# A vision tower with a Fourier mixer and a routed MLP: the last step in its own order, and unread products in TensorE's gaps

## What is computed

```python
h = h + attn(layernorm(h))     # x_proj * mod, then a convolution along the tokens by rfft/irfft, then out_w
h = h + ffn(layernorm(h))      # base matrix + shared low rank + 2 of 6 routed experts of rank 16

# attn: x_proj = x @ in_w + in_b ; mod = gelu(x @ mod_w1 + b1) @ mod_w2 + b2
#       y = irfft(rfft(x_proj * mod) * rfft(kernel)) ; y @ out_w + out_b
# ffn:  gate = softmax(x @ router_W.T + router_b); the two largest, renormalised, weight the experts
```

## Time and profile before

| what | value |
|---|---|
| median of 3 runs | 1279.57 us (1276.67, 1279.57, 1279.72) |
| the profiled execution | 1276.65 us, its span 1274.9 us |
| PE busy | 1228.7 us, 96% of the span |
| DVE busy | 872.7 us, 68% |
| ACT, POOL busy | 585.6 us (46%), 400.0 us (31%) |
| DMA | mean 45 GB/s |

### The profile page before, as it was taken

One profiled execution on the slowest core, in us unless ns is written; L12 is line 12 of the kernel. 1 busy time (PEld: TensorE's weight loads), 2 busy tenths in 40 slices (PEclk: granted clock), 3 DMA queues, 4 the chain that ended last, 5 costly groups with the idle time before them and its releaser, 6 DMA issues.

```text
span 1274.9 us, 21132 instructions
## 1 busy us (share of the span) xinstructions
PE 1228.7 (96%) x8148; PEld 1204.5 (94%) x8148; DVE 872.7 (68%) x2617; ACT 585.6 (46%) x1108; POOL 400.0 (31%) x462
## 2 busy tenths in 40 slices
PE   6999999999999999999999999999999999999954
PEld 5999999999999999999999999999999999999954
DVE  6467766667766666776766776666677666667665
ACT  6644544444444435444544545444444444453410
POOL 4632333232233323223333223332322333232100
PEclk9999999999999999999999999999999999999976
DMA  7111111101111110111110011111011111100000
GB/s 239 38 38 51 50 51 38 50 17 47 50 51 51 38 50 13 51 50 51 50 39 29 35 50 51 51 38 51 14 51 50 51 50 38 49 15 13 13 1 33
DMA packets 23182, 57.18 MB, mean 45 GB/s; under 512 B 2665, under 2 KB 18218, under 8 KB 19114
## 3 DMA queue, kind: packets, MB, share of 16 engines
q1 hardware_dynamic: 22266, 55.05, 12.4%
q10 hardware_dynamic: 816, 0.79, 0.2%
HBM read 42.98 MB, written 12.85 MB: 44 GB/s over the span
## 4 chain that ended last, share of the span: by engine, by line
PE 94%; DVE 4%; DMA 1%; POOL 1%; ACT 0%; issue 0%; ACTq 0%; DVEq 0%; POOLq 0%
PE rotating L956 17%; PE rotating L957 17%; PE rotating L958 17%; PE rows_ps L956 10%; PE rows_ps L957 10%; PE rows_ps L958 10%; PE turn L1098 5%; PE turn L1082 2%; PE turn L995 2%; PE rows_ps L1003 2%; PE turn L956 1%; PE turn L957 1%; PE turn L958 1%; PE rotating L1063 1%; DMA spec_y<-dram_tok_w 1%; POOL w_l L349 0%
## 5 line engine op out<-in xcount | busy, mean ns | idle before, releaser
L472 ACT ACTIVATE gelu<-rotating,biases 128x392 f32<-128x392 f32 x256 | 148.9, 582 | 203.8 <-PE rotating L958 203.6
L383 POOL TENSOR_TENSOR folded<-modulated 128x196 f32<-128x196 f32 x64 | 38.6, 603 | 566.4 <-DVE modulated L794 566.4
L370 POOL TENSOR_TENSOR gelu_l<-gelu,gelu_h 128x784 fp32r<-128x784 f32 x62 | 117.2, 1890 | 227.6 <-DVE norm L777 201.4
L355 POOL TENSOR_TENSOR patches_l<-patches,patches_h 128x384 fp32r<-128x384 f32 x186 | 184.4, 1019 | 0.5 <-ACT patches_h L430 0.5
L956 PE MATMUL rotating<-gelu_h,w_h 128*128 128x392 f32 x512 | 177.7, 347 | 0.0
L956 PE MATMUL rotating<-x_h,w_h 128*128 128x392 f32 x512 | 177.2, 346 | 0.0
L957 PE MATMUL rotating<-x_l,w_h 128*128 128x392 f32 x512 | 174.6, 341 | 0.0
L958 PE MATMUL rotating<-x_h,w_l 128*128 128x392 f32 x512 | 174.6, 341 | 0.0
L957 PE MATMUL rotating<-gelu_l,w_h 128*128 128x392 f32 x512 | 174.3, 340 | 0.0
L958 PE MATMUL rotating<-gelu_h,w_l 128*128 128x392 f32 x512 | 174.0, 340 | 0.0
L956 PE MATMUL rows_ps<-tokw_h,patches_h 128*128 128x256 f32 x576 | 165.2, 287 | 7.4 <-POOL patches_l L361 7.4
(11 more groups left out here) (205 smaller groups left out, 2951.9 us busy)
## 6 DMA issues: line engine op xcount, KB each, us to landing
patches<-dram_x_rest SPq DMA_DIRECT2D x31, 1152.0 KB, 5.1
out<-h_sb SPq DMA_DIRECT2D x32, 384.0 KB, 2.5
patches<-dram_x_first SPq DMA_DIRECT2D x3, 384.0 KB, 4.8
h_sb<-dram_x_second SPq DMA_DIRECT2D x1, 768.0 KB, 8.2
prod<-dram_tok_w ACTq DMA_DIRECT2D x2, 256.0 KB, 5.5
gelu<-dram_w SPq DMA_DIRECT2D x1, 512.0 KB, 6.7
norm<-dram_w SPq DMA_DIRECT2D x1, 384.0 KB, 6.2
gelu<-dram_w SPq DMA_DIRECT2D x1, 384.0 KB, 7.3
```

The lines of the kernel that those rows point to most:

```text
L355: pool.tensor_tensor(patches_l[:, k, :], patches[:, k, :], patches_h[:, k, :].bitcast(F32), ALU.subtract).then_inc(pool_patches_lo, 1)
L370: pool.tensor_tensor(gelu_l[:, 2 * j:2 * j + 2, :], gelu[:, 2 * j:2 * j + 2, :], gelu_h[:, 2 * j:2 * j + 2, :].bitcast(F32), ALU.subtract)\
L383: pool.tensor_tensor(folded[:, m, 0, :, 1:NF], fwd, back, ALU.add)
L472: act.activation(gelu[:, k, :], bank(g + 1, UP[k])[:, 0:GT], ACT.Gelu, bias=b1_bias[:, k:k + 1]).then_inc(act_gelu, 1)
```

## The change

The loop ends with step 31. Step 32 and the end are written out, in another order on every engine:

- TensorE does two chunks of the first down product ahead of `inverse_dft(last - 1)` and two of the second ahead of `mixer_tiles(last - 1)`. DVE makes the first half of `modulated` ahead of `add_mixer(last - 1)` and the second in the middle of the layer norm (`meanwhile`), where both stood behind that norm. `turn_fold(last)` goes ahead of `turn_x2(last - 1)`, and `dft(last)` ahead of `base_route(last - 1)`. DVE's `gelu_lo` moves ahead of `spectrum_of_y` and `finish`.
- `gate_exp` is cut in two, `gate_range` (7 instructions) and `gate_exp` (7), and the parts of the gate of round `last - 1` are spread over waits. ACT makes the norm of the last two tiles (`last_normalise`).
- The last five tiles have one gate instead of two (a gate of three tiles and one of two), in memory of its own (`GateRoom`, in the `patches` buffer), for which two small constants are loaded. Their router and expert products (102 columns) are apart from the base products (256 columns) and ahead of them; the routed products add onto the base products in three banks, each stored when it is done.
- `keep_clock(ps, n)` makes n products of 512 columns into a free bank. Nobody reads them. There are 8, 4, 2, 3, 9, 24, 8, 6 and 5 of them at nine places, 69 in all.

The core of the diff (the gate's functions otherwise only take their memory as an argument):

```diff
-            for i in range(1, GROUPS + 1):
+            for i in range(1, GROUPS):
                 if i + 2 < ROUNDS:
                     load_patches(i + 2)
+                else:
+                    sp.wait_ge(pool_patches_lo, KT * (ROUNDS - 2))
+                    sp.dma_start(last_thr, last_rank_thr_d).then_inc(last_consts, 16)
+                    sp.dma_start(last_bias, last_router_bias_d).then_inc(last_consts, 16)
                 if in_range(i - 3):
                     store(i - 3)
-            for d in range(GROUPS - 2, ROUNDS):
-                store(d)
-            sp.wait_ge(result_out, 16 * ROUNDS)
+            last = GROUPS - 1
+            store(last - 2)
+            store(last - 1)
+            first = output_tiles(last)[0]
+            for n, tiles in enumerate(LAST_BANKS):
+                sp.wait_ge(dve_result, last + n + 1)
+                at, slot = first + tiles[0], (first + tiles[0]) % H_SLOTS
+                sp.dma_start(out_v[:, at:at + len(tiles), :], h_sb[:, slot:slot + len(tiles), :])\
+                    .then_inc(result_out, 16)
+            sp.wait_ge(result_out, 16 * (last + len(LAST_BANKS)))
...
+            pool.wait_ge(gate_done, last - 1)
+            gelu_lo(last, 0)
+            gelu_lo(last, 1)
+            fold(last, 0)
+            fold(last, 1)
+            pool.wait_ge(pe_out, 2 * last + 3)
+            pool.memset(y_h[ROUTED:ROUTED + 1, 0, :].bitcast(F32), 1.0).then_inc(last_ones_row, 1)
...
+            def last_normalise():
+                act.wait_ge(dve_ln, LN_STEPS * (GROUPS + 3))
+                for t, j in enumerate(output_tiles(GROUPS)):
+                    ins = act.activation(norm1[:, t, :], h_sb[:, j % H_SLOTS, :], ACT.Identity,
+                                         bias=ln_tmp[:, 1, 0, t:t + 1], scale=ln_tmp[:, 0, 0, t:t + 1])
+                ins.then_inc(act_last_norm, 1)
...
+            gelu_hi(last, 3)
+            y_sine(last - 1)
+            y_hi(last - 1)
             fold_hi(last)
+            x2_hi(last - 1, rows_ps, x2_h)
             y_sine(last)
             y_hi(last)
-            gated_hi(last - 1, turn[:, 0])
+            last_normalise()
             x2_hi(last, turn, x2_h)
             x2_hi(last + 1, rotating, x1_h)
-            gated_hi(last, rotating[:, 2])
-            gated_hi(last + 1, rotating[:, 2])
+            gated_hi(last - 1, rotating[:, 2])
+            last_gated_hi()
...
+                if meanwhile:
+                    meanwhile()
...
+            gelu_lo(last, 2)
+            spectrum_of_y(last - 1)
+            gelu_lo(last, 3)
+            finish(last - 2, rows_ps)
+            whole_y(last - 1)
+            y_lo(last - 1)
+            dve.wait_ge(dve_y_lo, DH * last)
+            modulate(last, 0)
+            add_mixer(last - 1, rows_ps[:, 2], bank(GROUPS, OUT)[:, 0:DIM])
+            stats = stats2(last - 1, 1)
+            layer_norm_scales(GROUPS + 1, stats, slice(1, 2), 3, meanwhile=lambda: modulate(last, 1))
+            normalise(last - 1, norm2, 1)
             fold_lo(last)
+            x2_lo(last - 1, rows_ps, x2_h, x2_l)
             real_products(last)
             imaginary_products(last)
             spectrum_of_y(last)
-            gate_exp(last - 1, rows_ps)
+            gate_range(last - 1, round_routes, round_room)
             whole_y(last)
             y_lo(last)
-            gate(last - 1, rows_ps)
             add_mixer(last, rotating[:, 1], rotating[:, 2, 0:DIM])
+            stats2(last, 1)
             dve.wait_ge(pe_out, 2 * last + 3)
             slot = output_tiles(last + 1)[0] % H_SLOTS
             hs = h_sb[:, slot:slot + 2, :]
             dve.tensor_tensor(hs, rotating[:, 0].rearrange("p (t d) -> p t d", t=2), hs, ALU.add).then_inc(dve_h2, 2)
-            stats2(last, 1)
             stats = stats2(last + 1, 0)
             layer_norm_scales(GROUPS + 2, stats, slice(0, 2), 3)
             normalise(last, norm2, 1)
-            dve.wait_ge(pe_turn_gated, last)
-            normalise(last + 1, norm1, 0)
-            gated_lo(last - 1, turn[:, 0])
-            finish(last - 1, rows_ps)
+            gate_exp(last - 1, round_room)
             x2_lo(last, turn, x2_h, x2_l)
             x2_lo(last + 1, rotating, x1_h, x1_l)
-            gate_exp(last, rows_ps)
-            gate(last, rows_ps)
-            gated_lo(last, rotating[:, 2])
-            gate_exp(last + 1, turn)
-            finish(last, rows_ps)
-            gate(last + 1, turn)
-            gated_lo(last + 1, rotating[:, 2])
-            finish(last + 1, turn)
+            gate(last - 1, round_routes, round_room)
+            dve.wait_ge(last_consts, 32)
+            gate_range(last, last_routes, last_room)
+            gate_exp(last, last_room)
+            gated_lo(last - 1, rotating[:, 2])
+            gate(last, last_routes, last_room)
+            finish(last - 1, rows_ps)
+            last_gated_lo()
+            last_finish()
...
+            def last_routes_products():
+                pe.wait_ge(dve_x2_lo, DH * GROUPS + DH)
+                for t in range(LAST_TILES):
+                    hi, lo = (x2_h, x2_l) if t < 3 else (x1_h, x1_l)
+                    toks = slice(t % 3 * TILE, (t % 3 + 1) * TILE)
+                    for c in range(DH):
+                        ins = mm3(last_routes[:, t, :], hi[:, c, toks], lo[:, c, toks], wide_h[:, c, DIM:WIDE],
+                                  wide_l[:, c, DIM:WIDE], c == 0, c == DH - 1)
+                ins.then_inc(pe_route, 1)
+            def last_base_products():
+                for t in range(LAST_TILES):
+                    hi, lo = (x2_h, x2_l) if t < 3 else (x1_h, x1_l)
+                    toks = slice(t % 3 * TILE, (t % 3 + 1) * TILE)
+                    second = LAST_PLACES[t][1] == 1
+                    for c in range(DH):
+                        mm3(last_place(t), hi[:, c, toks], lo[:, c, toks], wide_h[:, c, 0:DIM], wide_l[:, c, 0:DIM],
+                            c == 0 and not second, c == DH - 1, onto_read=second)
+            def last_turn_gated():
+                pe.wait_ge(gate_done, GROUPS)
+                pe.wait_ge(dve_gated_lo, GROUPS - 1)
+                for t in range(LAST_TILES):
+                    ps = rotating[0:ROUTED, 2, t * TILE:(t + 1) * TILE] if t < 4 else turn[0:ROUTED, 1, 0:TILE]
+                    ins = pe.transpose(ps, last_room.gated[:, t, :], ident[:, :])
+                ins.then_inc(pe_turn_gated, 1)
...
+            def keep_clock(ps, n):
+                for _ in range(n):
+                    pe.matmul(ps[:, 0:BANK], w1_h[:, 0, 0:P], w1_h[:, 0, 0:BANK], start=True, stop=True)
...
+            pe.wait_ge(act_gelu, HC * last + 7)
+            mlp_down(last, 0, (0, 1))
+            inverse_dft(last - 1)
+            mlp_down(last, 0, range(2, HC))
+            pe.wait_ge(act_gelu, HC * last + 8)
+            mlp_down(last, 1, (0, 1))
+            pe.wait_ge(dve_result, last - 1)
+            pe.wait_ge(dve_y_lo, DH * last)
+            mixer_tiles(last - 1, rows_ps[:, 2], bank(GROUPS, OUT)[:, 0:DIM])
+            mlp_down(last, 1, range(2, HC))
+            free = bank(GROUPS, DOWN[0])
+            pe.wait_ge(dve_mod, DH * last + 1)
+            keep_clock(free, 8)
             turn_fold(last)
+            keep_clock(free, 4)
+            turn_x2(last - 1, rows_ps, norm2)
+            keep_clock(free, 2)
+            dft(last)
             base_route(last - 1, rows_ps, x2_h, x2_l)
-            dft(last)
+            keep_clock(free, 3)
             inverse_dft(last)
+            keep_clock(free, 9)
             pe.wait_ge(dve_mod, DH * last + 2)
             pe.wait_ge(dve_y_lo, DH * last + DH)
             mixer_tiles(last, rotating[:, 1], rotating[:, 2, 0:DIM])
             mixer_tiles(last + 1, rotating[:, 0], None)
-            turn_gated(last - 1, turn[:, 0])
+            keep_clock(turn[:, 1], 24)
+            turn_x2(last, turn, norm2)
+            pe.wait_ge(act_last_norm, 1)
+            turn_x2(last + 1, rotating, norm1)
+            pe.wait_ge(dve_h2, 2 * last + 4)
+            keep_clock(rotating[:, 2], 8)
+            last_routes_products()
+            turn_gated(last - 1, rotating[:, 2])
+            last_base_products()
             routed(last - 1, rows_ps)
-            turn_x2(last, turn, norm2)
-            turn_x2(last + 1, rotating, norm1)
+            keep_clock(rotating[:, 2], 6)
+            last_turn_gated()
             pe.wait_ge(dve_result, last)
-            base_route(last, rows_ps, x2_h, x2_l)
-            base_route(last + 1, turn, x1_h, x1_l)
-            turn_gated(last, rotating[:, 2])
-            routed(last, rows_ps)
-            turn_gated(last + 1, rotating[:, 2])
-            routed(last + 1, turn)
+            keep_clock(rows_ps[:, 0], 5)
+            last_routed()
```

255 lines of the change are left out of this document (187 added, 68 removed).

## The result

| kernel | median of its runs | lowest to highest | ratio to the kernel before |
|---|---|---|---|
| before | 1279.38 us (4 runs) | 1276.67 to 1279.72 | |
| changed | 1259.62 us (4 runs) | 1259.45 to 1259.82 | 0.9855 (0.9842 to 0.9868) |

The kernel before has one run more here than in the table ahead of the prediction. The change takes 19.8 us off the median; 1260.0 had been forecast, and 1256.5 to 1266. The profiled execution took 1259.82 us.

The account below looks back on a forecast made before the run. TensorE's work bounds the body; a four-engine chain, partly at low clock, bounds the last 75 us. Successive leads end at 18.2 us, giving 1258.45 from the profile or 1261.4 from the median: middle 1260.0, range 1256.5 to 1266.

Parts of the forecast that it names:

- Down products and fold: Step 32: down products fill PE's wait for spec_y, lead 1.3 us; half of `modulated` goes early, fold turn's lead 3.4.
- Transform, inverse, projection: Behind the fold: spectrum no longer behind 18 products, lead 5.4 us; inverse transform at full clock, projection's lead 7.2.
- Norm: From projection to norm: 3.8 us to L932, three stats run earlier, lead 10.0; 24 unread products charged 0.25.
- Norm to split: From norm to x_l: two norms on ACT, no routed products before the turn; x_l ends at 1238.5, lead 13.2 us.
- One gate for two: Last gates: one gate of five takes 7.0 us and ends at 1249.2 against 1268.21, lead 19.0.
- Rival 1: Router and expert products: 102 columns cost 0.25 us each, so PE ends them 3.9 later, 1264 us; chance 0.18.
- Last products: From the gate's end: 2.0 us, then 2.8 to the last sum, at 1254.1 against 1272.29, lead 18.2.
- rival 3: The end: unread products don't hold the clock, the lead becomes a loss of 12 us, 1288 or 1291; chance 0.025.
- Rival 2: The end's waits: one count of unread products is wrong, costing 3 to 5 us, 1263 to 1266; chance 0.10.
- Rival 4: The end: DVE stays late in part, costing half of the lead, 9 us, 1269; chance 0.06.
- The skill's rule: Ahead of the norm's turn: about 131 ns per unread product, 24 over after 3.1 us, span 1256.45; not adopted.
- The sum: Whole kernel: lead 18.2 us gives 1258.45 from the profiled execution, 1261.4 from the median; the middle, 1260.0, was forecast.

Follow-up runs that it names:

- e3: Changed kernel with step 32 in the old order, the new end kept and 75 unread products fitted to the old waits: 1262.79 us.
- e7: Changed kernel without the 24 unread products ahead of the last norm's turn, the other 45 kept: 1262.12 us.
- e4: Changed kernel with the gate of five tiles cut again into gates of three and two, one directly behind the other: 1265.46 us.
- e1: Changed kernel without its 69 unread products, order and waits kept: 1266.79 us.
- e2: Kernel before, in its old order, with 114 unread products added at ten places fitted to its waits: 1270.52 us.
- e9: The kernel of e8 with 18 more unread products, on a buffer of ones, ahead of the very first product: 1260.28 us.
- e5: Changed kernel with the last two tiles' norms on DVE again instead of on ACT: 1260.47 us.
- e6: Changed kernel with twice as many unread products at each of the nine places, 138 in all: 1271.66 us.
- e8: Changed kernel with 20 unread products added in the waits at 24 to 26 us (8) and 27 to 30 us (12): 1258.95 us.
- e10: The kernel of e9 with 6 more unread products, 2 ahead of `spectrum_products` and 4 behind: 1258.26 us.

## Why the prediction was right, step by step

**Down products and fold.** Forecast leads 1.3 and 3.4. The idle 1.32 us are gone and the down products fill them; the fold's turn has 3.2. The missing 0.2 is latency behind the last down product: 2.3 us pass from the row after it (1211.71) to the turn, where 2.05 had been reckoned. Undoing the step costs 3.2 us (e3), about what the lead says.

**Transform, inverse, projection.** 5.4 and 7.2 were forecast, 5.1 and 6.8 measured. Of the 0.4 missing, 0.25 is the delay handed on, and the rest is from the fold's turn to the spectrum (5.13 for 5.0). The inverse takes 2.03 instead of 3.73, as from the full-clock row.

**Norm.** Forecast 10.0, measured 9.3. From the projection to L1084 pass 3.88 us and from there to the norm 4.16, forecast 3.8 and 4.0. The 24 unread products were charged 0.25 and cost nothing: the turn starts 0.05 behind the norm (1236.71, 1236.66), just as it does without them (1236.41, 1236.36 in e7). Without them 2.5 us are lost; a smaller number was not tried.

**Norm to split.** 4.4 us were forecast and 4.0 measured, which gave 0.4 of the delay back. The 0.25 charged above is part of it. Another 0.25 is a slip in the sum: its terms from the norm at 1234.1 on (1.0, 0.25, 0.5, 0.5 and 1.9) end at 1238.25, and it went on with 1238.5.

**One gate for two.** The sum was 7.0 us and the row says 6.9. Its largest open price was that of a product of 102 columns: rows of the changed kernel are 0.11 us apart, 30 of them end in time for the gate at 3.6 us behind the first, and 0.12 had been taken. Rival 1 (0.25 each, 1264) falls. The gate of two lasted 5.5 us in e4; cut apart, the gates cost 4.8 us more, and with the clock 5.8.

**Last products.** Forecast 4.9 us from the gate to the last sum, 5.1 measured: 2.3 instead of 2.0 up to the first product, and 2.8 as forecast from there.

**The clock.** This was the premise of the sum, with rival 3 against it. The clock is 1.00 in every window from 40 us on; e1 and e2 price it at 7.2 us in the new order and 8.5 in the old, by the ends about 8 and 6.6. Rival 2 (one gap wrong) falls for the nine places of the end, where the clock never drops and no wait is over 0.7, but e7 and e9 show that its mechanism is real: a gap badly filled pulled the next unread products into the low clock. Rival 4 falls with the leads.

**The skill's rule.** The Trainium skill, TensorE: Matmul & The Clock Gate, section Back-to-back issue gap, would have the 24 unread products over after 3.1 us. They take 5.5 (1231.17 to the turn at 1236.71), 0.23 each, and the run follows the row.

**The sum.** 18.2 us of lead were forecast and 17.7 came (span 1274.9 + 0.82 - 1258.0). Against the median of before it is 19.8. The difference is the choice at the end of the prediction, the middle between a start from the low level of the kernel before and one from its median, 1258.45 and 1261.4. That the middle hit within 0.4 us was luck: the sum itself says 1258.45, and the profiled execution took 1259.82 because the lead was 0.5 short and the body 0.8 late, neither of which the prediction had.

What the late body is, the traces show. Ten profiled executions have nothing added at the start, and the clock is 1.00 in each of them from 40 to 1200 us. Their up product of step 32 starts between 1196.78 (e5) and 1198.50 (e6). Put in the order of the granted clock between 30 and 40 us (0.90, 0.88, 0.88, 0.86, 0.85, 0.84, 0.83, 0.81, 0.80, 0.73), that point comes at 1196.78, 1197.02, 1197.05, 1197.37, 1197.63, 1197.65, 1197.84, 1198.17, 1198.17 and 1198.50: the longer the clock stays low there, the later everything behind. With the clock held there the runs lie within 0.45 us (e8) and 0.3 (e10).

The two levels of the kernel before are another matter. In the three later groups it took 1276.8 to 1277.7 us with a mean clock of 0.984 and 1279.0 to 1280.1 with 0.981 to 0.982, and in the two groups of the changed kernel no such second level shows. Single runs of other kernels do stand apart with a clock of their own (0.994 instead of 0.997 in the slowest of e2 and of e5). So the time goes with the clock, but whether the upper level loses it in the start or in the end is open, since no trace of such a run was kept.

## What to carry to other kernels

Where a latency chain over several engines ends a kernel, count its dependent steps and not its bytes: two gates made one gave 4.8 us on DVE, and 5.8 with the clock behind it, since the narrower one takes 5.5 us for its 26 small instructions. Where TensorE waits in such a chain, work behind the wait pays for it a second time at the low clock, and unread products into a free bank win that back (6.6 to 8.5 us here) if they end just before what is waited for; each beyond that costs its 0.23 us. Fill the gaps in the order of time and look at the granted clock after each, since one that is left open makes the fillings behind it last longer (3.49 us for 2.09 in e7, 3.78 for 2.12 in e9) and can turn the gain of all into nothing (1260.3 against 1258.3 us, six products apart). Where kernels differ by less than their runs do, read the changed stretch in the traces from a common point on: that parted 60.6 from 60.1 us in e5, where the times did not.

## What the hardware showed that was not expected

**Going from 256 columns to 102 brings almost nothing.** F32R products of 102 columns go every 0.11 us, of 256 every 0.12, of 358 every 0.165 and of 512 every 0.23. So the 30 router products cost 3.4 us, where 102/256 of 0.12 each would have made 1.4. What sets this floor, and where between the two widths it begins, was not tried.

**A small DVE instruction beside POOL's.** Timeline of the changed kernel, both engines:

```profile
1212.69 0.61 POOL L436 TENSOR_TENSOR folded<-modulated 128x196 f32<-128x196 f32 x1 [5.05 <-DVE modulated L908]
1212.71 0.60 DVE L778 SCALAR_TENSOR_TENSOR ln_tmp<-ln_tmp 128x3 f32<-128x3 f32 x1
1213.37 0.60 POOL L438 TENSOR_TENSOR folded<-modulated 128x196 f32<-128x196 f32 x1
1213.42 0.57 DVE L781 TENSOR_TENSOR ln_tmp<-ln_tmp 128x3 f32<-128x3 f32 x1
```

Two instructions on three elements, of 0.17 and 0.16 us on twice as many elements elsewhere (at 1234.32 and 1234.60), took 0.60 and 0.57, each begun just behind one of POOL's and over with it. Between them L780, with a single source, took its 0.17. The Trainium skill, SBUF — State Buffer, section SBUF: two separate sides, says that a DVE instruction with two SBUF inputs and a GpSimd one that reads SBUF exclude each other for a whole instruction; these rows agree with it. It cost 0.84 us in a norm that nothing waited for at the time, but the change is what put this norm and POOL's fold side by side.

**The granted clock of the first microseconds.** The window from 5 to 10 us says 1.00, and the timeline of the changed kernel says

```profile
7.69 0.41 PE L1106 MATMUL rows_ps<-tokw_l,patches_h 128*128 128x256 f32 x1
7.90 0.41 PE L1107 MATMUL rows_ps<-tokw_h,patches_l 128*128 128x256 f32 x1
```

0.21 us apart where the same width later goes every 0.12. In e9, behind 18 unread products that start at 1.73, the same products go at the later pace:

```profile
7.94 0.28 PE L1107 MATMUL rows_ps<-tokw_h,patches_h 128*128 128x256 f32 x1
8.05 0.28 PE L1108 MATMUL rows_ps<-tokw_l,patches_h 128*128 128x256 f32 x1
```

So here the record of the clock does not show what the distance of equal products does, and at the start of a kernel the latter is the one to read.
